# Rotating the buffers of three stages in a fused attention and feed-forward layer: softmax tile order, two transpose banks for four, four output slots for two

## What is computed

```python
q, k, v = x @ Wq, x @ Wk, x @ Wv                  # x is layernorm(x)
att = softmax(einsum('bid,bkd->bik', q, k), axis=1)
out = tile(matmul(att, v), (1, 1, 16))            # x = x + out
...
x_prev = concat([zeros, x[:, :-1]])               # x is layernorm(x)
xr = mu_r * x + (1 - mu_r) * x_prev               # xk the same with mu_k
r = sigmoid(xr @ W_r.T)
k_act = square(relu(xk @ W_k.T))
out = r * (k_act @ W_v.T)                         # x = x + out
```

## Time and profile before

| | us |
|---|---|
| median of two runs | 734.13 |
| the two runs | 729.59 and 738.67 |
| the profiled execution, its own time | 724.43 |
| its span on the slowest core (core 5) | 722.8 |
| spans of the eight cores | 703.8 to 722.8 |

### The profile page before, as it was taken

One profiled execution on the slowest core, in us unless ns is written; L12 is line 12 of the kernel. 1 busy time (PEld: TensorE's weight loads), 2 busy tenths in 40 slices (PEclk: granted clock), 3 DMA queues, 4 the chain that ended last, 5 costly groups with the idle time before them and its releaser, 6 DMA issues.

```text
span 722.8 us, 5714 instructions; the slowest of 8 cores (703.8 to 722.8 us)
## 1 busy us (share of the span) xinstructions
PE 347.0 (48%) x1392; PEld 123.9 (17%) x1392; DVE 266.2 (37%) x483; ACT 294.6 (41%) x469; POOL 65.5 (9%) x61
## 2 busy tenths in 40 slices
PE   0004000004978877787762000000068999999794
PEld 0001000001431111111112000000023444444341
DVE  4802706237831011111121544423790002225766
ACT  3204004050029888889860366504663234330000
POOL 2000000000000030000000011000000000006685
PEclk9999655555995666666665555555587999999998
DMA  9965985865210089910000045184300000005786
GB/s 236 292 137 83 297 165 166 227 130 117 59 29 9 7 124 157 273 42 2 1 0 1 5 146 202 60 165 71 58 0 1 0 1 0 1 1 167 252 276 236
DMA packets 79044, 75.82 MB, mean 105 GB/s; under 512 B 59427, under 2 KB 59443, under 8 KB 78948
## 3 DMA queue, kind: packets, MB, share of 16 engines
q1 hardware_dynamic: 25700, 41.01, 17.7%
q0 software_dynamic: 10944, 23.93, 14.8%
q10 hardware_dynamic: 42368, 10.52, 9.4%
HBM read 47.79 MB, written 21.56 MB: 96 GB/s over the span
## 4 chain that ended last, share of the span: by engine, by line
PE 33%; DMA 19%; DVE 16%; ACT 11%; issue 10%; ACTq 7%; SPq 2%; DVEq 1%; POOL 0%; POOLq 0%
PE dpool L560 9%; PE ktp L966 8%; PE rps L926 7%; ACT p_sb L625 5%; ACTq L378 5%; DMA zdram<-zst 5%; DMA z1T<-z1dram 4%; DMA y_out<-x2b 4%; PE dpool L541 4%; DMA xst<-x_in 3%; DVE xk L905 3%; ACT zst L829 3%; DVE x2b L1083 2%; DVE sums L431 2%; ACTq L848 2%
## 5 line engine op out<-in xcount | busy, mean ns | idle before, releaser
L625 ACT ACTIVATE p_sb<-dpool,negm 128x1024 bf16<-128x1024 f32 x128 | 140.6, 1127 | 18.7 <-DVE ell L595 18.7
L926 PE MATMUL rps<-wrT,xr 128*128 128x512 bf16 x256 | 59.2, 396 | 148.9 <-DVE xr L898 138.9
L560 PE MATMUL dpool<-qrep,krep 64*128 64x512 bf16 x256 | 96.8, 543 | 40.2 <-ACT p_sb L625 32.7
L459 PE MATMUL qk<-zT,wqk 128*128 128x512 bf16 x64 | 18.5, 441 | 164.5 <-DVE qrep L490 99.5
L364 ACT ACTIVATE zst<-xst 128x1024 bf16<-128x1024 f32 x32 | 33.8, 1057 | 104.5 <-issue 92.1
L1023 PE MATMUL ops<-wvT,kaT 128*128 128x512 bf16 x256 | 56.5, 379 | 6.6 <-DVE tmp L1078 5.0
L926 PEld LDWEIGHTS rps<-wrT,xr 128*128 128x128 bf16 x256 | 25.8, 101 | 181.9 <-issue 154.3
L966 PE MATMUL ktp<-xk,wkT 128*128 128x512 bf16 x256 | 55.4, 379 | 1.3 <-ACT r_sb L939 1.3
L585 DVE TENSOR_REDUCE negm<-dpool 128x1 f32<-128x128 f32 x32 | 7.9, 286 | 123.3 <-PE dpool L560 123.3
L991 DVE TENSOR_TENSOR kaT<-kaT 128x512 bf16<-128x512 bf16 x32 | 13.6, 425 | 94.3 <-ACT kaT L982 94.2
L388 DVE TENSOR_SCALAR smean<-sums,cconst 128x4 f32<-128x4 f32 x12 | 2.7, 229 | 111.9 <-ACT zst L364 83.4
(11 more groups left out here) (84 smaller groups left out, 391.9 us busy)
## 6 DMA issues: line engine op xcount, KB each, us to landing
xst<-x_in SPq DMA_DIRECT2D x32, 512.0 KB, 9.0
xst<-x_in POOLq DMA_DIRECT2D x32, 512.0 KB, 6.7
zdram<-zst SPq DMA_DIRECT2D x32, 256.0 KB, 8.2
y_out<-x2b SPq DMA_DIRECT2D x16, 512.0 KB, 4.4
z1dram<-z1b SPq DMA_DIRECT2D x16, 256.0 KB, 3.4
wrT<-wrT_in POOLq DMA_DIRECT2D x1, 2048.0 KB, 19.0
wkT<-wkT_in POOLq DMA_DIRECT2D x1, 2048.0 KB, 31.6
wvT<-wvT_in POOLq DMA_DIRECT2D x1, 2048.0 KB, 44.3
```

What stands on the lines that cost most here:

```text
L459: t.matmul(qk[buf][:, :], wqk[:, ct * 128:(ct + 1) * 128], zT[ct][:, nch * 512:(nch + 1) * 512], start=(ct == 0), stop=(ct == CT - 1), ski ...
L560: t.matmul(units[u][:, cc * 512:(cc + 1) * 512], krep[64 * a:64 * (a + 1), kt * 128:(kt + 1) * 128], qrep[64 * a:64 * (a + 1), c * 512:(c ...
L625: sc.activation(p_sb[(kt + 1) % 4][:, s * 1024:(s + 1) * 1024], units[u][:, :], AF.Exp, bias=negm[:, kt:kt + 1], accum_out=ellp[:, 4 * (kt ...
L926: ins = t.matmul(r_ps[t_ % 3][:, hh * 512:(hh + 1) * 512], xr[ct][:, t_ * 128:(t_ + 1) * 128], wrT[:, ct * C + hh * 512:ct * C + (hh + 1) ...
```

## The change

Three things change, in three stages, and no instruction is added, removed or moved past another.

- **Stage D.** Key tile `kt` now uses `p_sb` number `kt % 4` (writer L625, readers L541, L570 and L605). Tile 0 thus writes `p_sb0`, and the wait on `SVT` stands before the first exponential and no longer before that of tile 3.
- **Stage E.** There are two PSUM tiles `tp` in place of four. A transpose waits for the copy two blocks before it.
- **Stage K.** `x2b` has four slots in place of two, with four semaphores. The multiplication waits for the output write of tile t-4, and no longer of t-2. `tmp32` keeps its two halves and their wait. SyncE's output writes come in the same order.

```diff
-        YSs = [e(nc.semaphore(f"YS{i}")) for i in range(2)]
+        YSs = [e(nc.semaphore(f"YS{i}")) for i in range(4)]
...
-        ys_k = lambda t: 16 * (t // 2 + 1)
+        ys_k = lambda t: 16 * (t // 4 + 1)
...
-                                     p_sb[(tt_ + 1) % 4][:, w * 512:(w + 1) * 512],
+                                     p_sb[tt_ % 4][:, w * 512:(w + 1) * 512],
...
-                            if kt == 3:
+                            if kt == 0:
                                 sc.wait_ge(SVT, 16)
...
-                        sc.activation(p_sb[(kt + 1) % 4][:, s * 1024:(s + 1) * 1024],
+                        sc.activation(p_sb[kt % 4][:, s * 1024:(s + 1) * 1024],
...
-        cm_tp = [nc.psum_tensor(f"tp{i}", [128, 64], F32) for i in range(4)]
+        cm_tp = [nc.psum_tensor(f"tp{i}", [128, 64], F32) for i in range(2)]
...
-                if b >= 4:
-                    t.wait_ge(SV, e_tpev(b - 4))
+                if b >= 2:
+                    t.wait_ge(SV, e_tpev(b - 2))
...
-                t.transpose(tp_ps[b % 4][:, :],
+                t.transpose(tp_ps[b % 2][:, :],
...
-                              tp_ps[b % 4][:, :]).then_inc(SV, 1)
+                              tp_ps[b % 2][:, :]).then_inc(SV, 1)
...
-                  nc.sbuf_tensor("x2b", [128, 2 * C], F32, side="right")]
+                  nc.sbuf_tensor("x2b", [128, 4 * C], F32, side="right")]
...
-                         in_=x2b[:, (t_ % 2) * C:(t_ % 2 + 1) * C]).then_inc(YSs[t_ % 2], 16)
+                         in_=x2b[:, (t_ % 4) * C:(t_ % 4 + 1) * C]).then_inc(YSs[t_ % 4], 16)
...
                 if t_ >= 2:
                     v.wait_ge(SV, k_x2(t_ - 2))
-                    v.wait_ge(YSs[t_ % 2], ys_k(t_ - 2))
+                if t_ >= 4:
+                    v.wait_ge(YSs[t_ % 4], ys_k(t_ - 4))
```

More of the change, by code:

```diff
@@ L605, in _ @@
                     v.tensor_copy(xp_sb[:, kt:kt + 1],
-                                  p_sb[(kt + 1) % 4][:, 4095:4096]).then_inc(SV, 1)
+                                  p_sb[kt % 4][:, 4095:4096]).then_inc(SV, 1)
                 if q + 2 < KT // 2:
@@ L1061, in _ @@
             for t_ in range(TOWN):
[L1062 to L1067, removed]
+                k_ydma_emit(sy, t_)
+            for s in range(4):
+                sy.wait_ge(YSs[s], 16 * (TOWN // 4))
         @block.vector
@@ L1082, in _ @@
                 v.wait_ge(SV, k_tmp(t_))
-                v.tensor_tensor(x2b[:, (t_ % 2) * C:(t_ % 2 + 1) * C],
+                v.tensor_tensor(x2b[:, (t_ % 4) * C:(t_ % 4 + 1) * C],
                                 tmp32[:, (t_ % 2) * C:(t_ % 2 + 1) * C],
```

## The result

| | us |
|---|---|
| with the change, median of 43 runs | 726.07 |
| before, median of 42 runs | 722.9 |
| ratio, 95% interval | 1.0041 (1.002 to 1.0061) |
| that is | +3.0 (+1.4 to +4.4) |
| forecast | +1.2, on a level of 734.13 |

The change made the kernel slower by a small amount that is clear of zero, and far inside 2%. The two runs shown ahead of the forecast lie at the slow end of what 42 runs gave, so their median, 734.13, on which the forecast stood, was some 11 us high for a reason that has nothing to do with the change.

A forecast was written before the change was run, and what follows sets the result against it. No single engine bounds the kernel: stages in series, each edit priced where it stands. 3.2 + 3.0 - 5.0 = +1.2 us on the two-run median of 734.13 gives 735.3 us, range 725 to 744.

The forecast's parts named there:

- Stage D, +3.2: First exponential: its table load stands behind the new wait for the v^T write and starts 3.2 us later, uncovered.
- Stage E, +3.0: Transposes: a round stays 0.81 us but carries two blocks, so 7 rounds in place of 3; 3.0 us added.
- Stage K, -5.0: Last stage: VectorE's 13.7 us of waits for output writes go, GpSimd's round is next; 5.0 us less.
- Its first part, the pace: Last stage: GpSimd goes at 3.68 us per tile, where core 5 had made 3.87 over fifteen steps.
- Its second part, the tail: End of last stage: last multiplication no longer behind GpSimd's last addition; 2.2 us less on core 4, expected on every core.
- my three candidates: Last stage, what is late next: TensorE at 3.48 us per tile, GpSimd's load round at 3.68, or mutually exclusive additions at 3.57.
- The choice between -6.0 and -2.2: Last stage: core 5 gains 6.0 us, core 4 2.2; the prediction took 5.0, as only the slowest core counts.
- The sum: Whole kernel: 3.2 + 3.0 - 5.0 = +1.2 us.
- Rival 2: Last stage: loads slow towards 5.4 us, GpSimd's round stays 3.87, only the 2.2 tail is gained; net +4.0, chance 0.20.
- Rival 1: Last stage: TensorE becomes the bound, 10.7 us less; net -4.5, 729.6 us, chance 0.10.
- Rival 3: Last stage: VectorE's addition holds up GpSimd's next, pace 4.14 us per tile; net +7.1, 741.2 us, chance 0.08.
- The row at 676.61: Last stage, core 5 before: VectorE's addition beside GpSimd's took 3.79 us in place of 1.22, read as VectorE yielding.

The follow-up runs named there:

- d_only: The kernel before with only stage D's new order of the softmax tiles: ratio 1.0041 against the kernel before.
- e_only: The kernel before with only stage E's two transpose tiles in place of four: ratio 1.0057 against the kernel before.
- k_short: k_only with output writes of 64 of the 1024 columns, the rest left unwritten: ratio 0.9863 against the kernel before.
- k_only: The kernel before with only stage K's four slots of x2b: ratio 0.996 against the kernel before.
- k_psum: k_only with the product multiplied in place in four PSUM tiles, so VectorE's addition reads one SBUF operand: ratio 0.9944 against the kernel before.
- k_ahead: k_only with GpSimd's loads of x_in issued three tiles ahead of its addition: ratio 1.0236 against the kernel before.
- b_ahead: The kernel before, two slots of x2b, with GpSimd's loads issued three tiles ahead: ratio 1.0253 against the kernel before.
- b_psum_ahead: The kernel before, two slots of x2b, with multiplication in place in PSUM and loads three tiles ahead: ratio 0.9935 against the kernel before.
- k_psum_ahead: k_only with multiplication in place in PSUM and loads three tiles ahead: 706.37 us against 719.75, ratio 0.9821.

## Why the prediction was wrong

- **Stage D, +3.2.** Right: 3.2 us on every core, +3.3 in the mean span of `d_only`. The table load did stand behind the new wait, and ScalarE's length of the stage did not change (159.4 us from first to last exponential on core 5, both before and after).
- **Stage E, +3.0.** Right: a round is 0.81 us with two blocks as with four, 3.0 us more on every core, +3.4 (error 0.6) in `e_only`.
- **Stage K, -5.0.** This step failed: the term was mis-sized, and what came is -2.3 in the mean span and -2.9 by the ratio. That VectorE's waits vanish was right, and that GpSimd's round comes next was right. Core 5's 6.0 us, which I leaned on, had two parts. The first did not come, and the second came by about half.
- **Its first part, the pace, some 2.9 us.** "So GpSimd's round is what is late next, at 3.68 per tile" took a length read from one execution as a constant to which core 5, at 3.87, would fall. It did not fall. The mean pace is 3.62 to 3.91 with the old stage and 3.75 and 3.78 with the new one, and core 5 went to 4.02. That length depends on how fast the loads land, and they share their time with the writes. On core 5 they landed after 5.9 us, which by my own formula (5.9 + 2.35) / 2 is 4.1 per tile, and `k_short` shows what the writes cost: without them the loads land at 4.0 and the pace is 3.34. Whether the four slots by themselves made the loads later, beyond that one core, is not shown.
- **Its second part, the tail, 2.2 us on core 4 and 3.1 on core 5.** "The last multiplication no longer stands behind the last GpSimd addition" holds on three of the eight cores in `k_only`. On the others VectorE is still held in the addition before by GpSimd's last one. The mean gain is 1.4 us, and only `k_psum`, which removes the exclusion, has the full tail of 2.5 us everywhere. I had the exclusion among my three candidates, but not in the tail.
- **The choice between -6.0 and -2.2.** I took core 5's figure, because the slowest core is the time. But core 5's slow stage belonged to that execution and was not a property of the kernel: with an unchanged stage K the other executions had 63 to 73 us on a core, and the longest was on core 4 once and on core 3 twice. What came is near the figure of core 4, -2.2. That it is so near is partly luck, as the tail alone gave 1.4.
- **The sum.** 3.2 + 3.0 - 2.9 = +3.3 against +3.0 (1.4 to 4.4) measured. Rival 2, with +4.0 and a chance of 0.20, had the right outcome, a tail gained and no shorter pace. Its cause, that a load would go from 4.5 towards 5.4 us, is seen on core 5 alone; `k_short` shows that writes do slow the loads, but not that they slow them more than before. Rival 1 was reached only with both cures. Rival 3's mechanism exists, but where it cost time, in `k_ahead`, its loser was VectorE. The row at 676.61, which the prediction says agrees with the rule on the port pair, agrees in the exclusion and not in who wins (see the last section).
- **The level.** 735.3 rested on a median of two runs; the profiled execution's 724.43 was the better guide, as 42 runs with a median of 722.9 show. The measured 726.07 lies near the low end of the stated 725 to 744, and says little for or against the three terms.

Left open: where the rest of the 2 to 3 us in stage K comes from beside the 1.4 of the tail. The pace varies from one execution to the next by more than that.

## What to carry to other kernels

When a wait for a buffer goes, the pace of the next candidate is not a constant of the old trace if it hangs on transfers: here the same instructions gave 3.6 to 3.9 us per tile from one execution to the next, and a gain of 0.2 per tile on one core is no forecast. Two engines that exclude each other can be kept apart by a wait that looks like waste: taking GpSimd's waits for its loads away alone cost 2.5% (`b_ahead`), and with the exclusion removed as well the kernel gained 0.65% (`b_psum_ahead`), or 1.8% with four slots (`k_psum_ahead`). And a small rotation of buffers is not free where one of them is still being read (3.2 us at the head of a stage), nor is halving the buffers of a ping-pong between two engines: its round time stays, and only the blocks in it halve.

## What the runs showed of the hardware

- An addition of VectorE with both operands in SBUF, beside GpSimd's, does not take turns with it: in `k_ahead` it waited through four GpSimd additions in a row (10.30 us for 1.22). With one operand in PSUM (`k_psum`) it took 1.22 us each of 16 times, beside the same GpSimd additions. The Trainium skill, SBUF — State Buffer, section "SBUF: two separate sides", gives the port pair to whichever instruction starts first, and exempts what does not read twice from SBUF. The exemption is what `k_psum` shows. The order of arrival is borne out only in part: VectorE's addition from 712.84 went ahead of GpSimd's from 712.96, but in the earlier trace rows VectorE's is recorded from 676.61, GpSimd's from 676.94, directly behind its issue of a load at 676.35, and VectorE lost. What makes the difference is open. No run shows VectorE getting its turn between two GpSimd additions that follow without a pause.
- Loads of 512 KB land later beside writes of 512 KB. In the mean of the cores the median landing was 4.0 us beside almost no writes (`k_short`) and 4.7 beside all of them (`k_only`). This is not the most that a core can move: with the loads issued three tiles ahead (`k_psum_ahead`) they landed after 7.3 us, and the same bytes went through in 57 us in place of 64.5.
